# Squared lengths in column groups, an expert's weights held as the stationary operand, and norms of two chunks with a row moved ahead of the second attention

## The chip, the cores and the metric

The kernel runs on one core of one Trainium2 chip. The metric is the device time of one execution in microseconds, given as the median of its runs. PE is TensorE (PEld its weight loads), DVE is VectorE, ACT is ScalarE, POOL is GpSimd, SP is SyncE. A float32 matmul shows as two PE instructions ("passes") in the trace.

## What is computed

A decoder of two layers over x (2 x 512 tokens of 256 features, so 1,024 rows or 8 chunks of 128 rows) and a context of 2 x 1,024 rows of 128. Each step is added to x. Cut to its skeleton:

```
x += performer(ln(x))              # L0: 16 heads of 64, exp(dn*q@P.T - |q|^2*dn^2/2 - max)
x += causal_attn(ln(x)) + cross_attn(ln(x), ctx)
x += moe_top2_of_8(ln(x))
x += retention(ln(x))              # L1
x += double_attention(ln(x), ctx)  # a1 on itself, then a2 on the context, each with an MLP
x += moe_top1_of_4(ln(x))          # silu(x@w_v[gate]) * (x@w_v[value]) @ w_proj
```

In the performer each query and key needs its squared length per head. In the last step each row goes to the one expert whose router logit is highest. Between a1 and a2 stands `ln(x)` with a gain and a shift, and a2 begins with a layernorm of that result.

## The kernel before

Every stage is a class with one program for each engine. The order is written out by hand: a generator (`order`, `lead_in`) gives the steps, and each engine walks through the same steps and does its own part. Engines meet at semaphores; PSUM's eight banks are handed out in turn (`Banks.open`), and PE waits there until the earlier content of a bank has been read.

**Performer** (`Performer`, L503 to L925). Two heads make a pair; eight pairs for keys, eight for queries. `project` (L682) makes a pair's 128 features by 1,024 rows, ACT keeps them (L806) and their squares `sq` (L807). `tensor_features` multiplies by P (L695) and then makes the squared lengths (L701): eight matmuls whose stationary operand is a 128 x 128 chunk of `sq` and whose moving operand `half` has two columns, so that the result stands by rows, 16 columns in one bank. DVE copies it (L849), before the maxima of the same pair, and for queries forms maximum and exponent's argument (L894 to L899). ACT takes the exponential (L788), POOL adds a constant (L627), and PE turns the result (L361), multiplies by the contexts (L747). Between them stand `contexts` (L731) and `values` (L711).

**Lead-in of a2** (`Mha` with cross, L2283 ff.). a1 ends with an MLP: `tensor_up` (L2527) for the first and the second half of the rows, ACT's GELU (L2589), `tensor_row` (L2536), eight matmuls for a chunk of rows. Chunks 0 to 3 are made in a1's own program, chunks 4 to 7 in a2's lead-in, between a2's first maxima (L1282 on PE, L1402 on DVE: a matmul of 512 columns and the maximum over them, 37 of them and one set of turned maxima L1295 before the attention proper begins). Each row gets its add and its statistics on DVE (L425, L265), then, for four chunks at once, variance, root (L282 on ACT, which needs its table loaded between GELUs), gain and shift (L299, L301, one chunk of four on POOL), then the next layernorm (L265 to L297, L307). `xturn` (L361) turns four normed chunks, ACT copies them with gain and shift (L377), and the queries' projection (L1456) and its two copies (L1462, L1463) follow. How many maxima go behind each piece of the lead-in stands in `beside`.

**Last stage** (`Swiglu`, L3173 ff.). DVE ranks the rows by expert, POOL scatters them to DRAM (L3189, L3193, eight each), SP loads them back in 11 tiles of 128 rows, each tile owned by one expert. Per tile: two transposes (L3230), eight up matmuls of 512 columns with the tile's rows as the stationary operand and the owner's weights, found by a register, as the moving one (L3245); ACT silu (L3284), DVE product (L3310); eight transposes of the product (L3256), one half copied by DVE (L3324), the other by ACT (L3295); eight matmuls with `w_proj` (L3266) for the tile before.

## Time and profile before

| | us |
|---|---|
| median of 3 runs | 1690.67 |
| runs | 1687.85 to 1697.34 |
| the profiled execution | 1698.3 |
| its span, first to last instruction | 1696.5 |
| PE busy | 1558.7 (92%) |
| DVE busy | 855.4 (50%) |
| ACT busy | 694.0 (41%) |
| POOL busy | 565.0 (33%) |

The performer lies at 13 to 205 us of the span, the second attention's lead-in at 1147 to 1217 us, the last stage's tiles at 1558 to 1688 us. A PE that is busy is not yet at its full pace: the trace gives the granted clock beside the busy time, 1.00 for 2.4 GHz and 0.50 for 1.2 GHz, and at 0.50 every matmul takes twice as long.

### The profile page before, as it was taken

The page shows a single profiled execution, that of the slowest core. Times are in us where ns is not written, and L with a number is a line of the kernel's source. Part 1 is how long each engine was busy: PE and PEld are TensorE (multiplying, and loading weights), DVE is VectorE, ACT ScalarE, POOL GpSimd, SP SyncE. Part 2 cuts the span into 40 slices and gives each one's busy share as a digit, 9 for nine tenths or more (in the row PEclk, how much of TensorE's full clock was granted, in tenths as well). Part 3 has the DMA queues.
Part 4 walks back from the last instruction along what each step waited for, and adds up shares of the span by engine and source line. Part 5 has one row for each costly group of instructions (what it writes and reads, how often), then busy time and mean ns, then how long its engine had stood idle before and what let it go on. Part 6 is the DMA issues. An engine that isn't in the chain of part 4 may idle for free.

```text
span 1696.5 us, 24207 instructions
## 1 busy us (share of the span) xinstructions
PE 1558.7 (92%) x9698; PEld 821.3 (48%) x9711; DVE 855.4 (50%) x1797; ACT 694.0 (41%) x1015; POOL 565.0 (33%) x689
## 2 busy tenths in 40 slices
PE   7999989999999988798689999998799999994997
PEld 5788863333323363575363333564233333573565
DVE  2255547499947654101674567423677774212221
ACT  3443322567654534321315445541355556421111
POOL 3043233610105433000311346440367778603000
PEclk9999998999999988899789899997799999996999
DMA  6000010000000028542500000130300000373000
GB/s 198 1 1 1 1 47 7 1 1 1 1 1 1 1 80 290 169 163 68 78 2 19 0 1 2 51 112 0 118 1 1 1 1 25 107 285 120 7 11 8
DMA packets 70339, 84.24 MB, mean 50 GB/s; under 512 B 24945, under 2 KB 55889, under 8 KB 69202
## 3 DMA queue, kind: packets, MB, share of 16 engines
q1 hardware_dynamic: 67395, 75.31, 13.9%
q0 software_dynamic: 2832, 7.38, 1.4%
q8 instruction: 77, 1.26, 0.3%
q14 instruction: 35, 0.29, 0.1%
HBM read 63.56 MB, written 19.51 MB: 49 GB/s over the span
## 4 chain that ended last, share of the span: by engine, by line
PE 83%; DVE 6%; DMA 3%; ACT 3%; issue 2%; POOL 2%; SPq 0%; ACTq 0%; POOLq 0%; DVEq 0%
PE psum L1310 13%; PE psum L1329 9%; PE psum L1282 6%; PE psum L3245 5%; PE psum L2536 4%; PE psum L682 3%; PE psum L1306 3%; PE psum L1351 3%; PE psum L2527 3%; PE psum L2102 3%; PE psum L1456 3%; PE psum L3266 2%; DVE a_nm L1402 2%; PE psum L361 2%; PE psum L2094 2%
## 5 line engine op out<-in xcount | busy, mean ns | idle before, releaser
L1402 DVE TENSOR_REDUCE a_nm<-psum 128x1 f32<-128x512 f32 x384 | 251.2, 685 | 148.9 <-PE psum L1282 109.2
L1402 DVE TENSOR_REDUCE xa_nm<-psum 128x1 f32<-128x512 f32 x256 | 162.0, 683 | 31.2 <-PE psum L1282 25.4
L1364 ACT ACTIVATE xnT<-psum 128x1024 f32<-128x1024 f32 (+3 forms) x104 | 94.9, 952 | 64.7 <-PE psum L1310 55.1
L1364 ACT ACTIVATE a_w<-psum 128x1024 f32<-128x1024 f32 x86 | 83.8, 1021 | 66.5 <-PE psum L1310 56.4
L1310 PE MATMUL psum<-xa_cq,xa_ckT 32*128 32x512 f32 x512 | 104.1, 587 | 0.0
L1282 PE MATMUL psum<-a2kr,a2qr 32*128 32x512 bf16 x256 | 85.6, 402 | 16.5 <-DVE a_nm L1402 15.7
L1310 PE MATMUL psum<-a2qT,a2kT 32*128 32x512 f32 x512 | 97.9, 605 | 0.0
L1282 PEld LDWEIGHTS psum<-a2kr,a2qr 32*128 32x128 bf16 x256 | 21.0, 91 | 125.4 <-DVE a_nm L1402 111.0
L3245 PE MATMUL psum<-sw_wv,sw_xgT 128*128 x176 | 80.1, 609 | 0.5 <-ACT sw_xgT L3289 0.3
L1282 PE MATMUL psum<-xa_ckr,xa_cqr 32*128 32x512 bf16 x256 | 74.0, 390 | 2.9 <-POOL xa_ckr L1502 2.1
L1399 DVE TENSOR_REDUCE xa_parts<-psum 128x4 f32<-128x512 f32 x80 | 53.8, 690 | 43.0 <-PE psum L1277 23.2
L1364 ACT ACTIVATE xn<-psum 128x1024 f32<-128x1024 f32 (+3 forms) x64 | 56.5, 922 | 44.7 <-PE psum L1310 41.0
L1364 ACT ACTIVATE xa_w<-psum 128x1024 f32<-128x1024 f32 (+3 forms) x64 | 56.2, 915 | 37.4 <-PE psum L1310 33.6
L1306 PE MATMUL psum<-a_mrow,onesb 3*128 3x512 bf16 x384 | 69.9, 397 | 1.5 <-DVE a_mrow L1415 1.1
L1306 PE MATMUL psum<-xa_mrow,onesb 3*128 3x512 bf16 (+3 forms) x384 | 67.7, 357 | 3.3 <-ACT xa_w L1364 0.8
L3310 DVE TENSOR_TENSOR sw_h<-sw_gt,psum 128x512 f32<-128x512 f32 x22 | 15.1, 688 | 85.8 <-PE psum L3245 85.8
L2102 PE MATMUL psum<-mo_w,mo_hT 128*128 128x256 f32 (+1 forms) x256 | 58.0, 380 | 0.0
L1282 PEld LDWEIGHTS psum<-xa_ckr,xa_cqr 32*128 32x128 bf16 x256 | 19.1, 91 | 77.7 <-DVE xa_nm L1402 68.2
L1282 PE MATMUL psum<-a1kr,a1qr 32*128 32x512 bf16 x128 | 46.5, 408 | 8.1 <-DVE a_nm L1402 8.0
L2149 DVE COPY mo_o<-psum 128x256 f32<-128x256 f32 (+1 forms) x16 | 6.7, 418 | 93.0 <-PE psum L2103 93.0
L2037 POOL DMA_INDIRECT mo_xs<-scratch_yo,mo_fro x16 | 15.2, 950 | 115.2 <-issue 113.7
L622 POOL TENSOR_SCALAR pf_kdd<-pf_kdd 128x1024 f32<-128x1024 f32 x8 | 22.2, 2772 | 93.3 <-ACT pf_kdd L783 93.1
(528 smaller groups left out, 3356.6 us busy)
## 6 DMA issues: line engine op xcount, KB each, us to landing
mo_w<-in_L_ffn_W SPq DMA_DIRECT2D x16, 1024.0 KB, 7.4
sw_wv<-in_L_ffn_w_v SPq DMA_DIRECT2D x4, 2048.0 KB, 18.7
scratch_a2v<-co_v SPq DMA_DIRECT2D x16, 256.0 KB, 2.2
scratch_a2k<-co_k SPq DMA_DIRECT2D x16, 256.0 KB, 3.4
a2kT<-scratch_a2k SPq DMA_DIRECT2D x8, 512.0 KB, 8.3
a2v<-scratch_a2v SPq DMA_DIRECT2D x4, 1024.0 KB, 11.6
sw_wp<-in_L_ffn_w_proj SPq DMA_DIRECT2D x4, 1024.0 KB, 19.3
a1li<-in_L_xattn_a_li_w SPq DMA_DIRECT2D x2, 1024.0 KB, 6.4
```

What stands on the lines that cost most here:

```text
L682: t = e.matmul(k.ps[:, bank, :], wt[:, f, chunk(pair)], k.xnT[:, f, cols(n)], start=f == 0, stop=f == FC - 1)
L1282: t = e.matmul(out, query[:, chunk(i)], key[:, part * S:(part + 1) * S], start=True, stop=True)
L1306: e.matmul(ps[:, pr + h % 2, lo:S], self.k.const.onesb[rows, :], self.mrow[n % 3][rows, lo:S], start=True, stop=False)
L1310: t = e.matmul(ps[:, pr + h % 2, lo:S], job.key(h)[:, chunk(c)], job.query(h)[:, lo:S], start=False, stop=True)
L1329: t = e.matmul(ps[32 * h:32 * h + 32, 6, lo:hi], job.value(c, h), self.weights(n, c)[:, h, lo:hi], start=start, stop=last and not upper)
L1351: t = e.matmul(ps[32 * h:32 * h + 32, 7, :], self.k.const.ones[:, 0:32], self.weights(n, c)[:, h, :], start=(n, c) == self.dens(n)[0], sto ...
L1364: e.activation(self.weights(n, c)[:, 2 * jj:2 * jj + 2, lo:S], ps[:, pr:pr + 2, lo:S], ACT.Exp, scale=self.scale).then_inc(*self.weighed.m ...
L1399: e.tensor_reduce(self.parts[n % 3][:, q, part, :], view.rearrange("p (h n) -> p h n", n=P), AX.X, ALU.max, negate=True).then_inc(*self.ma ...
L1402: e.tensor_reduce(self.nm[n % 3][:, q, part, h:h + 1], view, AX.X, ALU.max, negate=True).then_inc(*self.max_taken.mark(*i))
L2102: e.matmul(ps[0:n, bank, 0:D], hT[:, m, lo:lo + n], w2[:, m, :], start=m == 0, stop=False)
L2536: t = e.matmul(self.k.ps[:, self.k.banks.of(self.rows.name, c), 0:D], self.hT[:, m, chunk(c)], self.li3[:, m, :], start=m == 0, stop=m == ...
L3245: t = e.matmul(k.ps[:, bank, :], self.xgT[:, i, chunk(f)], self.wv[:, bass.ds(owner, 1), f, off:off + BANK].rearrange("p o n -> p (o n)"), ...
```

## The change

Three edits.

**Squared lengths.** `half` gets 32 columns (two of them filled) and becomes the stationary operand; the squares are the moving one, 256 columns in each of four matmuls that write to four groups of 32 partitions. The result stands by heads, not by rows, so ACT copies it to SBUF (`scalar_diagonal`, in the steps `keys` and `queries`, ahead of what these did), PE turns it with two transposes (a new step, `turn_diagonal`, placed behind the next projection for keys and behind the contexts for queries), and DVE copies the turned form. For queries DVE does that between the first and the second instruction of the pair's chain.

```diff
-        for c in range(NC):
-            w.wait_ge(*self.squared.at(which, pair, c // 4))
-            t = e.matmul(k.ps[:, bank, 2 * c:2 * c + 2], self.sq[i][:, chunk(c)], self.half[:, :], start=True, stop=True)
+        for j in range(4):
+            w.wait_ge(*self.squared.at(which, pair, j // 2))
+            t = e.matmul(k.ps[32 * j:32 * j + 32, bank, 0:D], self.half[:, :], self.sq[i][:, j * D:(j + 1) * D], start=True, stop=True)
         t.then_inc(*self.diagonal.mark(which, pair))
+
+    def tensor_diagonal_turn(self, e, w, which, pair):
+        k, kept = self.k, self.diagT[self.turn_of(which, pair) % 2]
+        bank = k.banks.of("pf_diagonal", which, pair)
+        w.wait_ge(*self.diag_kept.at(which, pair))
+        for i in range(2):
+            t = e.transpose(k.ps[:, bank, D + i * P:D + (i + 1) * P], kept[:, chunk(i)], k.const.ident[:, :])
+        t.then_inc(*self.diag_turned.mark(which, pair))
...
             elif step == "queries":
                 q = self.qp[i % 3]
+                self.scalar_diagonal(e, w, "q", i)
                 for n in range(2):
                     w.wait_ge(*self.query_scaled.at(i, n))
...
@@ order
                 yield "queries", pair + 1
+                if pair == 0:
+                    yield "turn_diagonal", ("q", 0)
             yield "contexts", pair
+            if pair + 1 < PAIRS:
+                yield "turn_diagonal", ("q", pair + 1)
```

PE where the performer's queries begin (projection of pair 2, features and lengths of pair 1, contexts of pair 0, turn of its queries), before:

```order
L682 MATMUL psum<-xnT,pf_wq 128x512 x4
L695 MATMUL psum<-pf_pbd,pf_hT 128x128 x8
L701 MATMUL psum<-pf_half,pf_sq 128x2 x8
L731 MATMUL psum<-pf_v,pf_kdd 128x130 x8
L361 MATMUL psum<-ident,pf_qp 128x128 x8
```

and in the changed kernel:

```order
L695 MATMUL psum<-xnT,pf_wq 128x512 x4
L708 MATMUL psum<-pf_pbd,pf_hT 128x128 x8
L714 MATMUL psum<-pf_sq,pf_half 32x256 x4
L723 MATMUL psum<-ident,pf_diagT 128x128 x2
L753 MATMUL psum<-pf_v,pf_kdd 128x130 x8
L723 MATMUL psum<-ident,pf_diagT 128x128 x2
L361 MATMUL psum<-ident,pf_qp 128x128 x8
```

The turn of pair 0's lengths stands behind pair 1's features, that of pair 1's behind the contexts; PE did neither before.

ACT at the same place (exponentials of queries and keys, then the next pair's copies and squares), before:

```order
L788 ACTIVATE pf_qp<-pf_qp 128x1024
L783 ACTIVATE pf_kdd<-pf_kdd 128x1024
L806 ACTIVATE pf_hT<-psum 128x512
L807 ACTIVATE pf_sq<-psum 128x512
L806 ACTIVATE pf_hT<-psum 128x512
L807 ACTIVATE pf_sq<-psum 128x512
L788 ACTIVATE pf_qp<-pf_qp 128x1024
```

and in the changed kernel:

```order
L827 ACTIVATE pf_diagT<-psum 128x256
L812 ACTIVATE pf_qp<-pf_qp 128x1024
L806 ACTIVATE pf_kdd<-pf_kdd 128x1024
L838 ACTIVATE pf_hT<-psum 128x512
L839 ACTIVATE pf_sq<-psum 128x512
L838 ACTIVATE pf_hT<-psum 128x512
L839 ACTIVATE pf_sq<-psum 128x512
L827 ACTIVATE pf_diagT<-psum 128x256
```

The copy of pair 1's lengths stands behind the exponential of pair 0's queries, the keys' exponential and four copies.

**Last stage.** Before each tile ACT and DVE copy the owner's `w_v` (256 x 2,048, one half of the features each, 2,048 columns on 128 partitions) into one of two buffers (a new one and the space of `xnT` and `ctxT`). The up matmuls take chunks of it as the stationary operand and the tile's rows as the moving one, 32 matmuls of 128 columns. The result already stands by hidden features, so the eight transposes and their two copies go, and DVE's product is the projection's input.

```diff
-                for f in range(FC):
-                    t = e.matmul(k.ps[:, bank, :], self.xgT[:, i, chunk(f)],
-                                 self.wv[:, bass.ds(owner, 1), f, off:off + BANK].rearrange("p o n -> p (o n)"), start=f == 0, stop=f == FC - 1)
+                for j in range(4):
+                    features = slice(off + j * P, off + (j + 1) * P)
+                    for f in range(FC):
+                        t = e.matmul(k.ps[:, bank, chunk(j)], self.own[i % 2][f][:, features], self.xgT[i % 2][:, chunk(f)], start=f == 0, stop=f == FC - 1)
...
+    def copy_own(self, e, w, i, f, copy, done):
+        w.wait_ge(*self.owned.at())
+        owner = e.value_load(self.owner_i[0:1, i:i + 1], min_val=0, max_val=E1 - 1)
+        for x in range(E1):
+            w.wait_ge(*self.experts.loads[f"v{x}"].at())
+        if i > 1:
+            w.wait_ge(*self.up.at(i - 2, 1, "value"))
+        copy(self.own[i % 2][f], self.wv[:, bass.ds(owner, 1), f, :].rearrange("p o n -> p (o n)")).then_inc(*done.mark(i))
```

**Lead-in of a2.** The norms behind a1's MLP (`out_norm`) and ahead of a2 (`norm`) take two chunks at a time; all chunks of the first are applied by DVE and none by POOL. In ACT's program the root of chunks 0 and 1 stands ahead of the second half's first GELU, that of 2 and 3 behind it, and the next norm's roots and applications behind all eight GELUs (before, two were left). Chunk 4 of the rows is made ahead of the first turn, the last norm stands behind a query's projection, and `beside` deals out the maxima anew: 12 instead of 18 up to the last row, 14 instead of 8 behind the last query.

```diff
-        pieces[4:4] = [("turn", 1)]
-        pieces[1:2] = [("row", (c, m)) for c in range(SC, NC) for m in range(HC)] + [pieces[1], ("norm", 4)]
-        return [("turn", 0)] + list(self.attention.lead_in(pieces, 0, 0, self.beside))
+        rows = lambda c: [("row", (c, m)) for m in range(HC)]
+        pieces[1:4] = rows(5) + rows(6) + [("norm", 4)] + rows(7) + [pieces[1], ("norm", 6), *pieces[2:4], ("turn", 1)]
+        return rows(4) + [("turn", 0)] + list(self.attention.lead_in(pieces, 0, 0, self.beside))
...
+        if step[0] == "row":
+            return step[1][1] % 2 if step[1] < (NC - 1, 4) else 0
+        if step[0] == "query":
+            return 2 if step[1] == (0, 0) else 3 * step[1][1]
+        return 2 if step[0] == "turn" else 0
```

PE in the second part of the lead-in (last rows, queries, second turn, up to the turned maxima), before:

```order
L2536 MATMUL psum<-a1li,a1hT 128x256
L1456 MATMUL psum<-xnT,a2wq 128x512 x4
L1282 MATMUL psum<-a2kr,a2qr 128x512 x2
L1456 MATMUL psum<-xnT,a2wq 128x512 x2
L1282 MATMUL psum<-a2kr,a2qr 128x512 x2
L361 MATMUL psum<-ident,ctxT 128x128 x8
L1282 MATMUL psum<-a2kr,a2qr 128x512
L1456 MATMUL psum<-xnT,a2wq 128x512 x2
```

and in the changed kernel:

```order
L2585 MATMUL psum<-a1li,a1hT 128x256 x4
L1491 MATMUL psum<-xnT,a2wq 128x512 x6
L361 MATMUL psum<-ident,ctxT 128x128 x8
L1317 MATMUL psum<-a2kr,a2qr 128x512 x2
L1491 MATMUL psum<-xnT,a2wq 128x512 x2
L1317 MATMUL psum<-a2kr,a2qr 128x512 x3
L1491 MATMUL psum<-xnT,a2wq 128x512 x2
L1317 MATMUL psum<-a2kr,a2qr 128x512 x3
```

The four maxima between the first half's queries are gone, and the second half's queries have three behind each instead of two.

ACT between the second half's first GELU and the first turn's copies, before:

```order
L2589 ACTIVATE a1hT<-psum,cols 128x512 x2
L282 ACT_TABLE_LOAD
L282 ACTIVATE a_norm_std<-a_norm_std 128x4
L2589 ACT_TABLE_LOAD
L2589 ACTIVATE a1hT<-psum,cols 128x512 x4
L282 ACT_TABLE_LOAD
L282 ACTIVATE a_norm_std<-a_norm_std 128x4
L307 ACTIVATE ctxT<-xn,a_norm_std 128x256 x2
L2589 ACT_TABLE_LOAD
L2589 ACTIVATE a1hT<-psum,cols 128x512 x2
```

and in the changed kernel:

```order
L2638 ACTIVATE a1hT<-psum,cols 128x512
L282 ACT_TABLE_LOAD
L282 ACTIVATE a_norm_std<-a_norm_std 128x2
L2638 ACT_TABLE_LOAD
L2638 ACTIVATE a1hT<-psum,cols 128x512 x7
L282 ACT_TABLE_LOAD
L282 ACTIVATE a_norm_std<-a_norm_std 128x2 x2
L307 ACTIVATE ctxT<-xn,a_norm_std 128x256 x2
```

No table load stands ahead of the last two GELUs any more.

## Rows read from the trace of the kernel before

**Rows 1.** Busy time of the engines in one stretch, with TensorE's granted clock.

```profile
89.00:200.00 111.00, 110.73 (x857) 99.01 (x856) 65.91 (x173) 42.84 (x68) 41.56 (x15) 1.00 0.00 1
```

**Rows 2.** PE timeline, one pair of the first attention's queries (start, us, engine, line).

```profile
123.37 1.95 PE L695 MATMUL psum<-pf_pbd,pf_hT 128*128 128x128 f32 x16
125.15 1.84 PE L701 MATMUL psum<-pf_half,pf_sq 128*128 128x2 f32 x16
126.86 2.04 PE L731 MATMUL psum<-pf_v,pf_kdd 128*128 128x130 f32 x16
128.73 1.91 PE L361 MATMUL psum<-ident,pf_qp 128*128 128x128 f32 x16
130.48 3.74 PE L711 MATMUL psum<-pf_wv,xnT 128*128 128x128 f32 x32
134.05 1.95 PE L747 MATMUL psum<-pf_bd,pf_qpT 128*128 128x130 f32 x16
```

**Rows 3.** PE timeline of the third attention: four column groups, and what follows.

```profile
983.59 0.64 PE L1329 MATMUL psum<-xnT,a1v 128*32 128x256 f32 x8
984.17 0.39 PE L1282 MATMUL psum<-a1kr,a1qr 32*128 32x512 bf16 x1
```

**Rows 4.** DVE timeline in the same pair as rows 2.

```profile
127.04 0.17 DVE L849 COPY pf_diag<-psum 128x16 f32<-128x16 f32 x1 [4.48 <-PE psum L701]
...
131.80 0.68 DVE L384 COPY pf_qpT<-psum 128x512 f32<-128x512 f32 x1
```

**Rows 5.** Timeline of DVE, POOL and ACT where the queries begin.

```profile
92.49 1.23 DVE L879 SCALAR_TENSOR_TENSOR pf_kdd<-pf_kdd,pf_diag 128x1024 f32<-128x1024 f32 x1
93.55 2.80 POOL L627 TENSOR_SCALAR pf_qp<-pf_qp 128x1024 f32<-128x1024 f32 x1 [5.79 <-ACT pf_qp L788]
93.75 1.06 ACT L783 ACTIVATE pf_kdd<-pf_kdd 128x1024 f32<-128x1024 f32 x1 [0.28 <-DVE pf_kdd L879]
...
95.19 0.59 ACT L807 ACTIVATE pf_sq<-psum 128x512 f32<-128x512 f32 x1
```

**Rows 6.** PE timeline of the second attention's lead-in.

```profile
1150.10 1.53 PE L361 MATMUL psum<-ident,ctxT 128*128 128x128 f32 x8 [2.98 <-ACT a1hT L2589]
1152.59 3.75 PE L1456 MATMUL psum<-xnT,a2wq 128*128 128x512 f32 x4 [0.96 <-ACT xnT L377]
...
1159.26 2.07 PE L2536 MATMUL psum<-a1li,a1hT 128*128 128x256 f32 x4
...
1171.60 1.13 PE L2536 MATMUL psum<-a1li,a1hT 128*128 128x256 f32 x4
...
1197.74 1.20 PE L1282 MATMUL psum<-a2kr,a2qr 32*128 32x512 bf16 x2 [6.00 <-DVE a_nm L1402]
...
1217.25 0.61 PE L1295 MATMUL psum<-identb,a_np 128*128 128x128 bf16 x4
```

**Rows 7.** ACT timeline in that lead-in.

```profile
1150.82 1.63 ACT L377 ACTIVATE xnT<-psum,cols 128x512 f32<-128x512 f32 x2 [0.77 <-PE psum L361]
```

**Rows 8.** Busy time and clock in three stretches, columns as in rows 1.

```profile
1156.00:1171.00 15.00, 14.31 (x30) 6.96 (x29) 5.60 (x9) 2.37 (x3) 0.00 (x0) 0.50 0.00 0
...
200.00:206.00 6.00, 4.53 (x30) 3.71 (x31) 3.08 (x10) 2.24 (x3) 0.00 (x0) 1.00 0.00 0
619.00:623.00 4.00, 2.55 (x14) 1.57 (x13) 2.35 (x7) 1.16 (x3) 0.22 (x1) 0.82 0.00 0
```

**Rows 9.** Chain that ended last, in order of time: a tile of the last stage.

```profile
1649.83 6.87 PE psum L3245 x16
1656.70 3.45 PE psum L3266 x16
1661.24 6.87 PE psum L3245 x16
```

**Rows 10.** PE timeline, the last tile's projection.

```profile
1684.07 3.72 PE L3266 MATMUL psum<-sw_wp,sw_hT 128*128 x16 [0.43 <-DVE sw_hT L3324]
```

**Rows 11.** POOL timeline, the first of eight row scatters ahead of the last stage.

```profile
1541.43 1.12 POOL L3189 DMA_INDIRECT scratch_swx<-xn,sw_to  x1 [7.26 <-DVE sw_owner L3380]
```

More of the change, by code:

```diff
@@ L303, in scalar_apply @@
     def scalar_apply(self, e, w, g):
-        for c in range(g, g + 4):
+        for c in range(g, g + self.size):
             if self.of(c) in "ab":
@@ L311, in pool_apply @@
         step = self.k.pool
-        for c in range(g, g + 4):
+        for c in range(g, g + self.size):
             dst = self.dst[:, c, :]
```

152 lines of the change are left out of this document (81 added, 71 removed).

## The prediction, on record before the changed kernel ran

> **What bounds the kernel now.** I read the page first: PE is busy for 92% of the span, so a microsecond counts where PE works or waits. Then busy time and clock by stretch, since a busy PE at 0.50 does half the work: in the performer's queries PE is busy 110.73 of 111.00 us at 1.00 [rows 1], so there every pass that goes is won and every new wait is lost. In the second attention's lead-in it is waits and the clock: PE waits 2.98 us for a GELU and 0.96 us for the turned chunks [rows 6], then does 15 us at 0.50 [rows 8], and later waits 6.00 us for DVE, which has all four chunks' norms ahead of the maxima [rows 6]. In the last stage the chain runs on PE alone, a tile every 1661.24 - 1649.83 = 11.41 us [rows 9].
>
> **Squared lengths, the pass itself.** Now 126.86 - 125.15 = 1.71 us a pair [rows 2]. The nearest row to the new form is a value product of four column groups with 256 columns: eight passes, and the next instruction starts 0.58 us later [rows 3]; so the groups run beside each other. A transpose costs (130.48 - 128.73) / 16 = 0.11 us [rows 2], two 0.22. New 0.80, saved 0.91, over 16 pairs **14.6 us**. If the groups ran one after another, eight passes of 256 columns at 3.72 / 16 = 0.23 us [rows 10] make 1.86, with the turn 2.08, and 16 pairs would lose 5.9 us; that end of the bounds is far from rows 3.
>
> **Its new waits.** PE's turn waits for ACT's copy, and DVE's chain for the turn. For keys the turn is a projection (3.5 us) behind, and ACT's copy, shorter than the 0.59 of 512 columns [rows 5], is done: no wait. For a query pair in the steady state, counted from the start of its features [rows 2]: features to 1.78, lengths to 2.36, contexts to 4.1, turn to 4.36, sixteen transposes to 6.1, values to 9.7; there `output` needs DVE's copy of the turned queries. Before, DVE's chain began at 127.04 - 123.37 = 3.67 and that copy ended at 132.48, 9.1 [rows 4]. Now the chain begins at about 4.55, its first maximum (0.6) done already, so the copy ends at 3.67 to 4.55 later less 0.6, about 9.4, and PE wants it at 9.7 instead of 134.05 - 123.37 = 10.7. It fits, with 0.3 us left.
>
> The **first query pair** doesn't fit. Its turn stands behind pair 1's features, and DVE's chain, ACT's exponential and everything that ACT has behind it hang on it. From that turn's end: DVE's chain for both halves 2.8 us; ACT's exponential 1.06 beside DVE's scaling of the next keys (0.23 + 1.23, done at 4.3); ACT's keys' exponential 1.06 to 5.4; four copies and squares at some 0.5 to 7.4; the copy of pair 1's lengths 0.4 to 7.8 [rows 5]. PE has only the contexts, 1.8 us, until it needs that copy. So PE stands for about **6.0 us**, once. POOL's 2.80 [rows 5] ends inside it. After a stand of that length the clock is likely to be at 0.50: after the 6.00 us wait it was at 0.50, and in the lead-in it took work of several us to come back [rows 6, 8]. Passes of some 5 us at 0.50 cost **2.7 us** more (bounds 0 and 7, half the 15 us of rows 8). The performer: 14.6 - 6.0 - 2.7 = **5.9 us** saved.
>
> **Last stage.** The eight transposes of a tile go: 8 x 0.11 = 0.88 us, 11 tiles, 9.7 us, and at the end the 0.43 us in which PE waits for a copy of the last [rows 10]. The up matmuls stream the same columns in 64 passes of 128 instead of 16 of 512. The same alternation of a new 128 x 128 stationary chunk and 128 moving columns is in `values`: (134.05 - 130.48) / 32 = 0.112 us a pass [rows 2], 64 make 7.14 against 6.87 [rows 9], 0.27 a tile, 3.0 us in all. Left: 9.7 + 0.4 - 3.0 = 7.1. No row shows a copy of 2,048 columns: ACT's 1,024 take 1.06 [rows 5], so some 2.0, DVE's 1,024 with two operands 1.23, so at most 2.4. A tile lasts 10.8 us, and each buffer is free for one whole tile ahead: hidden. The first two copies of DVE fall where POOL issues the eight scatters that PE waits for, and the first of those, beside small DVE work, took 1.12 us [rows 11]. Bounds 0 and 2 x 2.4 = 4.8 us; I take 1.5, since the copies are two and not all of each hits a scatter. Last stage **5.6 us** saved.
>
> The Trainium skill, SBUF — State Buffer, "SBUF: two separate sides", says more sharply that a float32 `tensor_copy` of VectorE from SBUF to SBUF keeps GpSimd from writing its DMA descriptors until it ends. By that rule both copies would be paid whole and, by their length at one column a cycle, the scatters come up to 4.8 us late; I keep it as a rival.
>
> **Lead-in.** From PE's end of the second up projection (1150.10 - 2.98 = 1147.12) to the turned maxima (1217.25) it now takes 70.1 us [rows 6]. The new course at clock 1.00: ACT has no table load ahead of its last GELUs any more, so the last follows PE's end by its own length and a hop, about 0.9 us (512 columns take 0.59 without a function's extra [rows 5]); row 3.5; the first norm, from DVE and ACT, is ready as the row ends; turn 0.9; ACT's two copies (1.63, the first beside the turn [rows 7]) leave a wait of 1.35; query 1.8; its copy 0.75: 9.2 us. Then two maxima, ten groups of two row matmuls and a maximum at 1.38 (1.13 and what follows [rows 6]) and four row matmuls, 16.1; DVE's gain and shift for two chunks hold up its maxima by 1.9 once. Three queries 5.4, a wait of 1.2 for the last norm, turn and two maxima 1.5, a wait of 0.8. Four queries with three maxima each: the third waits for a bank, 3.3 us each, 13; then 14 maxima at DVE's pace of 0.6 (0.68 for 512 columns [rows 4], a little overlapped), 8.4. Sum 57 us, 13 saved. The clock takes some back. At the second turn PE waits, turns and waits again as before, and will do some 7 us at 0.50, 3.5 us. At the first turn it is open: waits of 0.9, 1.35 and 0.75 with eight transposes between. Of two stretches with transposes between short waits, one fell (619 to 623, mean 0.82) and one held (200 to 206, 1.00) [rows 8]. If it falls there, rows and maxima run at 2.5 us a group (2.07 and its maximum [rows 6]) instead of 1.38, five or six groups long, 6 us. So 10 us saved if it holds, **4 us** if it falls. I take the fall, since three waits follow each other here.
>
> **Sum.** 5.9 + 5.6 + 4 = 15.5 us: 1682.8 against the profiled execution's 1698.3, and **1675.2** against the median of 1690.67, since the profiled run lay 7.6 above it and nothing in the sum is a share of the time.
>
> **Rivals.** (a) The clock holds at the first turn: 10 instead of 4, **1669**. For it: no wait is over 1.4 us, against 2.98 now. (b) DVE's later chain is seen in every query pair, not in one alone: only 0.3 us is left, and with 0.9 us more in the strided copy or in semaphores PE waits in 7 pairs, 6 us, **1681**. Against it: hops in rows 2 and 4 are about 0.2. (c) DVE's copies hold POOL whole (4.8 instead of 1.5) and the lead-in gives nothing, since its 14 last maxima are DVE's and the clock is low: 5.9 + 2.3 + 0, **1682.5**. (d) On the other side: the column groups don't run beside each other. Its place is L714, its price 16 x (2.08 - 0.80) = 20.5 us, **1696**; it decides from about 1.7 us a pair for lengths and turn, where the performer's gain is gone and the 8.7 of the first pair stay. Against it stand rows 3. (e) The change does less than it says: the first query pair costs more than is won in all, say 15 us of stand and low clock: 1681.5.
>
> **How the numbers follow.** Forecast (the fall at the first turn) 0.42, 1670 to 1680; (a) 0.27; (b) 0.10; (c) 0.10; (d) 0.05; (e) 0.06. Within 0.5% (8.5 us, about what a measurement of this kernel can tell from no change) are 1682.2 to 1699.1: half of (c), part of (b) and (e) and of (d), with some spread of the median; over that a part of (d). Faster 0.81, same 0.15, slower 0.04. The range takes in (a) with POOL unhindered below and (c) with a worse clock above: 1663 to 1687.
>
> **What would show it.** In the changed kernel's trace: lengths start 0.58 us ahead of the next PE instruction; one PE wait of about 6 us (on ACT) behind the contexts of pair 0 and no others in the performer; key pairs at 6.1 us instead of 7.0, query pairs at 15.0 instead of 15.9; tiles at 10.8 us; scatters longer than now only under DVE's copies; the wait of 2.98 gone to below 1 us, that of 6.00 to about 1.2; the clock in the first rows at 0.50 (forecast) or 1.00 (a). Wrong would be: waits in each query pair, tiles above 11.4, or a lead-in of 70 us.

## The result, and the profile after

The changed kernel's median is **1674.95 us** (1663.90 to 1689.80, 20 runs) against 1689.26 us of the kernel before beside it (1683.65 to 1699.57, 20 runs). The ratio of the two is 0.9909, with a 95% interval of 0.9886 to 0.9933: 15.4 us less, and 1675.2 was predicted. The profiled execution took 1671.95 us with a span of 1670.2 us, 26.3 us less than the span before. Runs at a low clock that lie over 1.5% above the fastest of their kernel (one here, three of the joined kernel's twelve in experiment 1, one of ten in experiment 4) are kept in the medians and means below; without its one the median here is 1674.69 us.

So the two traces show 26 us and the medians 14 to 15. That gap is the first thing to explain, for a sum that comes out right may hold terms that don't. I cut both traces at the same landmarks and read length and granted clock of every stage. Four stages are touched:

| stage | before, us | after, us | saved | forecast |
|---|---|---|---|---|
| performer, 0 to the projection behind it | 239.0 | 233.2 | 5.8 | 5.9 |
| lead-in, from the MLP's start to a2's attention | 114.2 | 104.6 | 9.6 | 4 |
| last stage, from the first up projection to the end | 138.1 | 128.6 | 9.5 | 5.6 |
| all others | 1205.2 | 1203.8 | 1.4 | 0 |

(The 5.6 holds 1.5 us for POOL's scatters, which lie ahead of that stretch; for the stretch itself the sum had 7.1.)

**Performer.** First the PE timeline of the changed kernel where the queries begin and in a later pair (start, us, engine, line, output and inputs, count; in brackets idle time before it and what ended it).

```profile
87.63 0.44 PE L723 MATMUL psum<-ident,pf_diagT 128*128 128x128 f32 x2
89.26 2.06 PE L753 MATMUL psum<-pf_v,pf_kdd 128*128 128x130 f32 x16 [1.19 <-DVE pf_qp L934]
...
95.49 0.44 PE L723 MATMUL psum<-ident,pf_diagT 128*128 128x128 f32 x2 [4.17 <-ACT pf_diagT L827]
...
96.82 5.19 PE L733 MATMUL psum<-pf_wv,xnT 128*128 128x128 f32 x32
101.85 1.95 PE L769 MATMUL psum<-pf_bd,pf_qpT 128*128 128x130 f32 x16
...
107.07 1.95 PE L708 MATMUL psum<-pf_pbd,pf_hT 128*128 128x128 f32 x16
108.95 0.64 PE L714 MATMUL psum<-pf_sq,pf_half 128*32 128x256 f32 x8
109.52 2.06 PE L753 MATMUL psum<-pf_v,pf_kdd 128*128 128x130 f32 x16
...
122.17 1.95 PE L708 MATMUL psum<-pf_pbd,pf_hT 128*128 128x128 f32 x16
```

The lengths are followed 0.57 us later by the next instruction (108.95 to 109.52), as [rows 3] had it, where [rows 2] show 1.71; the turn behind the contexts takes 0.22. A pair lasts 122.17 - 107.07 = 15.10 us. Against that stand one wait of 4.17 us on ACT's copy of the lengths and one of 1.19 us on DVE, 5.4 in all. Behind them the turn of eight chunks takes 0.18 us longer, and the values 101.85 - 96.82 = 5.03 instead of 3.57: the clock fell to half there and cost 1.6 us. No other full pair waits. One price is hidden in these rows: the features ahead of the lengths now take 108.95 - 107.07 = 1.88 us, where [rows 2] have 125.15 - 123.37 = 1.78. So a pair is 0.81 us shorter and not 0.91, 13.0 us in all instead of 14.6, and 13.0 - 5.4 - 1.6 = 6.0 us is what the stage shows (5.8). This is ACT's timeline at that place, with the first and the last of what stands in front of the copy, the keys' exponential and four copies and squares:

```profile
90.82 1.06 ACT L812 ACTIVATE pf_qp<-pf_qp 128x1024 f32<-128x1024 f32 x1 [8.66 <-DVE pf_qp L934]
...
93.12 0.58 ACT L838 ACTIVATE pf_hT<-psum 128x512 f32<-128x512 f32 x1
...
95.03 0.41 ACT L827 ACTIVATE pf_diagT<-psum 128x256 f32<-128x256 f32 x1
```

**Lead-in.** PE's timeline of the changed kernel, which answers [rows 6]:

```profile
1140.52 3.72 PE L2585 MATMUL psum<-a1li,a1hT 128*128 128x256 f32 x16 [0.78 <-ACT a1hT L2638]
...
1149.27 1.13 PE L2585 MATMUL psum<-a1li,a1hT 128*128 128x256 f32 x4
...
1150.65 1.13 PE L2585 MATMUL psum<-a1li,a1hT 128*128 128x256 f32 x4
...
1159.00 0.38 PE L1317 MATMUL psum<-a2kr,a2qr 32*128 32x512 bf16 x1 [1.71 <-DVE a_nm L1437]
...
1173.53 1.07 PE L361 MATMUL psum<-ident,ctxT 128*128 128x128 f32 x6 [1.34 <-DVE ctxT L297]
...
1177.21 3.75 PE L1491 MATMUL psum<-xnT,a2wq 128*128 128x512 f32 x4 [2.29 <-ACT xnT L377]
...
1200.26 0.61 PE L1330 MATMUL psum<-identb,a_np 128*128 128x128 bf16 x4
```

The wait of 2.98 us is 0.78, that of 6.00 has become two, of 1.71 and 1.34, and a group of two row matmuls and a maximum takes 1150.65 - 1149.27 = 1.38 us from the first one on: the clock did not fall at the first turn. From the second up projection's end to the turned maxima it is 1200.26 - 1139.74 = 60.5 us instead of 70.1. One wait is larger than planned: 2.29 us on the second turn's copies. ACT's timeline shows why:

```profile
1173.18 0.60 ACT L307 ACTIVATE ctxT<-xn,a_norm_std 128x256 f32<-128x256 f32 x1 [0.96 <-DVE a_norm_std L290]
1173.69 0.58 ACT L1497 ACTIVATE a2qr<-psum 128x512 bf16<-128x512 f32 x1
...
1175.60 1.47 ACT L377 ACTIVATE xnT<-psum,cols 128x512 f32<-128x512 f32 x2
```

The copies of two finished queries (L1497, L1498) stood in ACT's queue behind the application of the last norm (L307), which itself waited for DVE, and the turn's copies (L377) behind them.

**Last stage.** The chain of work that ended last in the changed kernel, in order of time (start, us, engine, what, line, count), which answers [rows 9]:

```profile
1561.05 7.15 PE psum L3295 x64
1571.87 7.15 PE psum L3295 x64
...
1654.54 6.92 PE psum L3306 x32
```

The timeline of the changed kernel with the first of DVE's two copies and POOL's scatters beside it, which answers [rows 11]:

```profile
1525.83 1.40 POOL L3240 DMA_INDIRECT scratch_swx<-xn,sw_to  x1 [0.31 <-issue]
1525.89 1.23 DVE L3334 COPY sw_own<-sw_wv 128x2048 f32 x1 [1.24 <-issue]
...
1527.54 1.55 POOL L3240 DMA_INDIRECT scratch_swx<-xn,sw_to  x1 [0.30 <-issue]
1529.39 0.96 POOL L3240 DMA_INDIRECT scratch_swx<-xn,sw_to  x1 [0.30 <-issue]
```

A tile takes 1571.87 - 1561.05 = 10.82 us against 11.41 in [rows 9], and the last two projections follow each other without a wait. The two scatters under DVE's copies took 1.40 and 1.55 us, one beside nothing 0.96. ACT's own copy of 2,048 columns took 1.91 us and DVE's 1.23, which was at most 2.4 in my bounds. The scatter of 1.40 us ends at 1527.23, 0.11 us after DVE's copy beside it (1525.89 + 1.23 = 1527.12).

### The profile page after: what moved, and what is told of

Same layout as the page of the kernel before. It is cut to its first block, busy times and chain, and to the rows that moved or that the text cites. A ratio compares the mean times of both kernels' runs of the same rounds, so it can differ in the third digit from the quotient of the medians.

```text
span 1670.2 us, 24916 instructions
## 1 busy us (share of the span) xinstructions
PE 1529.4 (92%) x10055; PEld 831.6 (50%) x10055; DVE 861.7 (52%) x1811; ACT 713.0 (43%) x1035; POOL 564.7 (34%) x683
## 4 chain that ended last, share of the span: by engine, by line
PE 84%; DVE 7%; ACT 3%; issue 2%; DMA 2%; POOL 1%; DVEq 0%; POOLq 0%; ACTq 0%; SPq 0%
PE psum L1345 13%; PE psum L1364 9%; PE psum L1317 6%; PE psum L3295 5%; PE psum L695 4%; PE psum L2585 3%; PE psum L1341 3%; PE psum L2576 3%; PE psum L1386 3%; PE psum L2137 3%; PE psum L1491 3%; DVE a_nm L1437 2%; PE psum L3306 2%; PE psum L2129 2%; PE psum L733 2%
## 5 line engine op out<-in xcount | busy, mean ns | idle before, releaser
L1345 PEld LDWEIGHTS psum<-xa_cq,xa_ckT 32*128 32x128 f32 x512 | 50.1, 193 | 3.2
L2159 ACT ACTIVATE mo_hT<-psum,cols 128x154 f32<-128x154 f32 x64 | 21.4, 386 | 70.6 <-PE psum L2129 70.6
L1399 ACT ACTIVATE ctxT<-psum 128x1024 f32<-128x1024 f32 x40 | 38.9, 1021 | 29.1 <-PE psum L1345 24.1
```

The costliest lines, as they stand in the source:

```text
L1345: t = e.matmul(ps[:, pr + h % 2, lo:S], job.key(h)[:, chunk(c)], job.query(h)[:, lo:S], start=False, stop=True)
L1399: e.activation(self.weights(n, c)[:, 2 * jj:2 * jj + 2, lo:S], ps[:, pr:pr + 2, lo:S], ACT.Exp, scale=self.scale).then_inc(*self.weighed.m ...
```

## Experiment 1: each edit alone

Three kernels, each the kernel before with one of the three edits as shown in the section on the change, and the changed kernel beside them on the same chip, so that all share the 35 runs of the kernel before (median 1691.77 us).

> The squared lengths' edit alone, on the kernel before. My sum has 5.9 us saved: 14.6 for 16 pairs, less one stand of some 6 us at the first query pair and 2.7 us of work at half clock behind it; the changed kernel's own trace shows 5.4 us of waits and some 1.7 us of half clock there, so 7.5 us by those rows. If instead each pair's passes save less than they seem, because DVE's and ACT's work is the limit, the whole gain is under 3 us and waits stand in the query pairs.

> The last stage's edit alone. My sum has 5.6 us saved. The two profiled executions put the stretch from 0.1 us ahead of the first up projection to the end at 9.5 us less, so the rival theory is that the gain is some 9 us: 11 tiles at 0.6, the last hidden turn's 0.9 and 0.4, 1.3 at the first tile and 1.5 between the first two. By the first theory POOL's two held scatters take 1.0 to 1.5 us of it back, by the second they only take 0.5.

> The lead-in's edit alone. My forecast had 4 us saved with the clock at half after the first turn, the rival 10 us with the clock held. The changed kernel's trace shows the clock held and 9.6 us. If the held clock belongs to this edit, the rows of chunks 5 to 7 run at 1.00 here too and 9 to 10 us are saved; if it was luck of that one execution (a clock that holds in some and falls in others), they run at 0.50 and about 4 us are saved.

> The changed kernel with all three edits, on the same chip as the three alone. If the edits don't meet, its saving is the sum of the three alone; by my sum 15.5 us, by the traces of stretches 7.5 + 9.5 + 9.6 = 26.6 us, by the medians of 20 runs 14.3 us. A sum of the three alone well over the joined one would show that one edit's gain is given back where another is made.

| kernel | median, us | ratio to before | 95% interval |
|---|---|---|---|
| lengths alone | 1690.95 | 0.9993 | 0.9972 to 1.0015 |
| last stage alone | 1681.79 | 0.9934 | 0.9913 to 0.9956 |
| lead-in alone | 1691.85 | 1.0000 | 0.9972 to 1.0028 |
| joined | 1677.38 | 0.9917 | 0.9883 to 0.9952 |

Only the last stage gives about what its stretch shows (8 to 11 us; the expectation of 9 holds against my 5.6, which lies outside the interval of 7.4 to 14.7). The lengths give 1 us where the stretch in their own trace is 5 us shorter, and the lead-in none, though its trace has the same 104.6 us as the changed kernel. Something outside the edited code takes the gain back. By the ratios the three alone add up to 12.3 us and the joined kernel saves 14.0 (8.1 to 19.8), so no gain is lost where the edits meet, and the 26.6 us of the stretches are not there.

## What takes the gains back: the clock in stages that nobody touched

Each run comes with the mean granted clock of its span, and within one kernel the times follow it closely: through all kernels that were timed, 0.01 of clock goes with 14.2 us (a line with one slope for all; 13.2 in the kernel before alone). So I compare the kernels once as they are and once at the same clock, 0.948, by that slope:

| kernel | mean, us | mean clock | at 0.948, us | difference at 0.948 |
|---|---|---|---|---|
| before (three sets, 80 runs) | 1689.7 to 1691.3 | 0.9485 to 0.9493 | 1691.6 to 1692.0 | 0 |
| lengths alone | 1690.8 | 0.9441 | 1685.3 | -6.6 |
| last stage alone | 1681.4 | 0.9497 | 1683.9 | -8.0 |
| lead-in alone | 1690.0 | 0.9495 | 1692.1 | +0.2 |
| changed kernel (20 and 12 runs) | 1675.6, 1680.4 | 0.9485, 0.9450 | 1676.3, 1676.1 | -15.7 |

The 95% intervals of the fourth column are 0.5 to 1.1 us wide on either side. At equal clock the lengths save 6.6 us, close to the 5.9 of the sum; the clock then takes most of it back. The lead-in is the opposite: its stretch has the clock at 0.85 before and at 0.94 after, so what it saves there is largely clock itself, and nothing is left at equal clock. (The comparison has a bias: idle time at half clock lowers the mean too, so a kernel with more of it looks a little better in the last column than it is. Experiment 4 has the size: 5.4 us more of waiting show as 2.3 at equal clock. The new lead-in has less waiting, so its +0.2 is likely too high.)

Where the clock differs, the traces show stage by stage. To see which stages move without any edit, I profiled the kernel before a second time.

> The kernel before once more, for a second trace of the same code. Its first trace lay 7.6 us above its median. If that is the clock in stages that the change doesn't touch, this trace differs from the first by whole steps in some of them (the attention's entry 75.0 or 68.8 us, the expert tiles 125.2 or 127.7, retention 73.4 or 75.5), each with its clock, and not in the others; if it is a drift of everything, all stages differ by the same share.

Busy time by stretch (from : to, us, then busy us of PE, PEld, DVE, ACT, POOL with instructions, clock, DMA). The kernel before, first trace: entry of the third step, expert tiles, last stage.

```profile
238.98:313.96 74.98, 72.08 (x201) 27.99 (x201) 56.48 (x129) 21.32 (x33) 32.91 (x51) 0.88 0.12 30
692.89:818.38 125.49, 106.80 (x573) 78.42 (x573) 22.72 (x51) 27.92 (x74) 13.26 (x14) 0.92 0.34 111
1558.43:1696.50 138.07, 128.68 (x458) 78.83 (x458) 27.43 (x45) 24.55 (x44) 13.33 (x14) 0.96 0.08 27
```

The same three stretches in the second trace of that kernel:

```profile
239.58:308.40 68.82, 66.19 (x199) 26.52 (x200) 55.80 (x129) 21.24 (x33) 32.90 (x51) 0.97 0.14 33
688.56:816.29 127.73, 109.08 (x572) 80.82 (x573) 22.73 (x51) 27.98 (x74) 13.28 (x14) 0.90 0.34 108
1555.74:1692.30 136.56, 127.18 (x458) 78.39 (x458) 27.42 (x45) 24.55 (x44) 13.71 (x14) 0.97 0.09 29
```

The same code took 74.98 us at 0.88 or 68.82 us at 0.97; 125.49 at 0.92 or 127.73 at 0.90; 138.07 at 0.96 or 136.56 at 0.97; and all 288.8 us of the attention between them are equal to 0.1 us. So these are whole steps in single stages, as the first theory had it, and no drift. The other traces take the same steps: retention 73.4 (0.92) or 75.4 (0.88), a1's attention 136.5, 138.0 or 140.0. Retention and the first attention (288.8 to 291.8) take their steps with and without the edits alike. Two steps go mostly with the lengths' edit, though it touches no line there. The expert tiles are at 127.5 us or more in nine of ten traces that have it, and at 125.1 to 125.5 in three of four without it: some 2 us given back for the 5.8 won. And the old lead-in takes 111.6 us in both traces with it, 114.2 or 114.3 in the three without: as much won again. The largest step of all, the entry's 6.1 us, is at its high level in two of four traces without the lengths' edit, in five of seven with it, and in none of the three with the earlier turn of experiment 2. That may be a part of it, but with so few traces it is a suspicion; what takes the lengths' gain back stays open.

**The lead-in's courses.** With the new lead-in the clock held through the rows in three traces (104.6 us each). In two (106.2 us each) it fell behind DVE's wait of 1.71 us for some 4 us, so that the next two groups of row matmuls took 1.87 and 1.76 us instead of 1.13. In two others with the same lead-in code (111.3 and 111.4) it fell there and stayed at half to the last row. The old one took 114.2, 114.2, 114.3, 111.6 and 111.6. Here is one that fell, PE's timeline of the first kernel of experiment 4:

```profile
1162.86 0.39 PE L1317 MATMUL psum<-a2kr,a2qr 32*128 32x512 bf16 x1 [1.71 <-DVE a_nm L1437]
...
1164.88 2.08 PE L2585 MATMUL psum<-a1li,a1hT 128*128 128x256 f32 x4
...
1167.41 2.08 PE L2585 MATMUL psum<-a1li,a1hT 128*128 128x256 f32 x4
```

The code up to here is that of the changed kernel and so is every wait before it (0.78, 1.19, 0.69, 1.71), yet from 1163 on two row matmuls and a maximum take 1167.41 - 1164.88 = 2.53 us instead of 1.38. And the attention behind it suffers too. In the changed kernel's trace and then in this one, 16 and 36 us at the place where the lead-in ends and the attention begins, and the whole attention (columns as above):

```profile
1196.00:1212.00 16.00, 14.50 (x62) 5.33 (x63) 10.25 (x18) 3.98 (x4) 7.87 (x13) 0.50 0.00 1
1201.78:1437.96 236.18, 227.29 (x1792) 74.77 (x1785) 157.18 (x254) 132.50 (x143) 176.92 (x164) 0.98 0.02 6
```

```profile
1206.00:1242.00 36.00, 33.54 (x143) 10.83 (x147) 20.65 (x33) 9.91 (x10) 16.90 (x20) 0.50 0.00 1
1212.44:1456.25 243.81, 234.55 (x1792) 75.91 (x1785) 157.51 (x254) 132.49 (x143) 176.94 (x164) 0.94 0.02 5
```

The first stretch of each is at 0.50. The changed kernel leaves half clock some 11 us into the attention and needs 236.2 us for it, as the kernel before does; this one stays there until 1242 and needs 243.8. So the best course saves 9.6 us, and the worst saves 2.8 and loses 7.6: 5 us slower than the kernel before. (The two losses need not come together: in experiment 6 the clock fell in the rows to their end, and the attention took 236.3 us.) From 1691.3 the best and the worst course make 1681.7 and 1696.1, and the twelve runs of the lead-in alone split in just that way, six from 1676.8 to 1689 (mean 1684) and six from 1694 to 1700.5 (mean 1696). I have a trace of the first kind of this kernel and of the second kind only of kernels with the other edits beside it, so that the split has this cause is likely and not shown. What decides which course an execution takes stays open.

**From 26 to 15.** The two profiled executions differ by 26.3 us. Of that, 1.5 is the last stage's step and 4.8 are those of retention and what follows it, both high in the first trace of the kernel before; 3.1 went the other way, the first attention's 291.8 in the changed kernel. The expert tiles were at 125.2 in the changed kernel's trace, where nine of ten have 127.5 or more: 2.5. The lead-in is at 104.6 and keeps its pace behind, where the mean over seven traces is 107.0 and (243.8 + 240.8 - 2 x 236.2) / 7 = 1.7 in the attention, against 113.2 with the old lead-in instead of 114.2: a saving of 4.5 instead of 9.6, 5.1 less. 26.3 - 1.5 - 4.8 + 3.1 - 2.5 - 5.1 = 15.5, where the ratio gives 15.4. I chose these steps knowing what had to come out, and retention's is as high in the second trace of the kernel before, so this is a plausible account and no proof.

## Experiment 2: an earlier turn for the first query pair

```diff
                 if pair + 2 < PAIRS:
                     yield "project", ("q", pair + 2)
-                yield "queries", pair + 1
                 if pair == 0:
                     yield "turn_diagonal", ("q", 0)
+                yield "queries", pair + 1
```

> The changed kernel with the first query pair's turn of lengths ahead of pair 1's features instead of behind them. My theory of the stand: DVE's chain and all that ACT has behind it hang on that turn, so with the turn 2.4 us (features and lengths) earlier and those 2.4 us of work to lie beside the chain, the stand of 5.4 us shrinks by 2.4 + 0.2 to some 3 us, and with it the half clock behind it: 3 to 4 us faster than the changed kernel. The rival: the stand belongs to ACT's queue itself (copies and squares of pair 2 ahead of the copy of pair 1's lengths), and stays at 5 us wherever the turn is.

> The squared lengths' edit alone, with the first query pair's turn earlier. The edit alone gave 0.8 us where I had 5.9. Theory one: the performer's stage gives what its trace shows (6.0 us at the start, 1.8 given back at the queries), and the rest is lost to lower clocks in later stages whose code is the same (2.3 us in the expert tiles); with the stand 2.7 us shorter this one gains 2.7 to 3.5 us more, 1687. Theory two: the stand itself is nothing that the time sees, because something later absorbs it; then it stays at 1691.

Once in the changed kernel: median **1668.04 us**, ratio to before 0.9896 (0.9874 to 0.9918), and at equal clock 3.1 us below the changed kernel. Once with the lengths alone: 1685.98 us, ratio 0.9974 (0.9948 to 0.9999) instead of 0.9993 (3.2 us), at equal clock 2.9 us less, so theory two (nothing moves) is unlikely. PE's timeline of the first of the two:

```profile
93.08 0.69 PE L723 MATMUL psum<-ident,pf_diagT 128*128 128x128 f32 x2 [3.08 <-ACT pf_diagT L827]
...
95.26 4.10 PE L733 MATMUL psum<-pf_wv,xnT 128*128 128x128 f32 x32
99.20 1.95 PE L769 MATMUL psum<-pf_bd,pf_qpT 128*128 128x130 f32 x16
```

One wait of 3.08 us in place of 4.17 + 1.19, and values in 3.94 us instead of 5.03, with 128.5 us for the queries instead of 131.2. The stand is real, it hangs on the turn's place as the sum had it, and the rival (it stays wherever the turn is) has fallen. What is left of it is ACT's queue: exponential, exponential, four copies and squares, then the copy of pair 1's lengths.

## Experiment 3: the column groups

```diff
-            t = e.matmul(k.ps[32 * j:32 * j + 32, bank, 0:D], self.half[:, :], self.sq[i][:, j * D:(j + 1) * D], start=True, stop=True)
+            t = e.matmul(k.ps[0:32, bank, 0:D], self.half[:, :], self.sq[i][:, j * D:(j + 1) * D], start=True, stop=True)
```

> The changed kernel with all four matmuls of the squared lengths written to the same 32 partitions instead of to four groups, so that they can't run beside each other; three quarters of the lengths are then lost and the output is wrong in that part. By my bounds the eight passes last 1.86 us one after another instead of 0.57: 1.3 us more a pair, 16 pairs, 20 us slower, and the key pairs last 7.4 instead of 6.2. If the 0.57 came from something else than the groups (32 columns of stationary operand that load quickly), the passes stay near 0.6.

PE's timeline of this kernel, the lengths of a query pair and what follows:

```profile
98.74 1.91 PE L714 MATMUL psum<-pf_sq,pf_half 128*32 128x256 f32 x8
100.58 0.44 PE L723 MATMUL psum<-ident,pf_diagT 128*128 128x128 f32 x2
```

The same eight passes last 1.84 us (98.74 to 100.58) when they write to one group and 0.57 when they write to four, and nothing else differs. The bound for the rival of serial groups was 1.86. The key pairs together took 78.8 us instead of 68.4 and the queries 141.4 instead of 131.2, 20.6 us in all where 20.5 was its price. The one run took 1708.94 us, 34 us above the changed kernel's median; the rest of that lies in the clock's steps of other stages, the attention's 240.8 us among them.

## Experiment 4: DVE's copies and POOL's scatters

```diff
         self.vector_places(e, w)
+        w.wait_ge(*self.loads["scatter"].at(NC - 1))
         self.vector_own(e, w, 0)
```

The second kernel puts eight more copies of the same size ahead of DVE's own, back to back:

```diff
     def vector_own(self, e, w, i):
+        if i == 0:
+            ...
+            for n in range(8):
+                w.wait_ge(*self.k.vec.now())
+                e.tensor_copy(self.own[1][1], self.wv[:, 0, 1, :]).then_inc(*self.k.vec.mark())
```

> The changed kernel with DVE's first two copies of weights held until the eight scatters have landed. If the copies cost the scatters 0.44 + 0.59 us, these take 0.96 to 1.1 each again, the first tile's turn comes 1.0 us earlier against POOL's first scatter (15.5 us as in the kernel before, not 16.0 to 16.5), and the kernel is 1 us faster or the same within the measurement. If it was something else that made two scatters long, they stay long and nothing moves. The copies then end some 1 us ahead of the first turn, so no wait is added.

> The changed kernel with eight more copies of 2,048 columns on DVE ahead of its first two, back to back: extra work that leaves the result alone. DVE then copies for about 12 us beside POOL's eight scatters. If a copy holds POOL until it ends, as my rival (c) and the Trainium skill's page SBUF — State Buffer have it, no scatter ends while copies follow each other (or one slips in between two copies, 1.2 us each at least), and the first tile's turn comes some 8 to 11 us later. If a scatter under a copy takes 0.44 to 0.59 us longer, as two did in the changed kernel's trace, eight or so are 0.5 longer: 3 to 4 us later. Each us of that is a us of the time.

POOL's and DVE's timeline in the first kernel, a scatter ahead of the copies and one beside them:

```profile
1546.37 0.96 POOL L3240 DMA_INDIRECT scratch_swx<-xn,sw_to  x1 [0.30 <-issue]
...
1556.48 1.45 POOL L3244 DMA_INDIRECT scratch_swr<-x,sw_to  x1 [0.30 <-issue]
1556.59 1.23 DVE L3334 COPY sw_own<-sw_wv 128x2048 f32 x1 [12.67 <-issue]
```

DVE's and POOL's timeline in the second kernel, where ten copies lie beside the scatters:

```profile
1516.64 10.06 DVE L3346 COPY ctxT<-sw_wv 128x2048 f32<-128x2048 f32 x8
1518.29 2.22 POOL L3240 DMA_INDIRECT scratch_swx<-xn,sw_to  x1 [0.31 <-issue]
...
1530.53 0.96 POOL L3240 DMA_INDIRECT scratch_swx<-xn,sw_to  x1 [0.30 <-issue]
```

With the copies behind, the scatters take 0.96, and those two of the next eight that now lie beside the copies take 1.45 and 1.69. From POOL's first scatter to PE's turn it is 15.10 us instead of 16.02: the two copies cost 0.9 us. The other traces agree: 15.99 to 16.08 in six with the copies beside the scatters, 14.90 to 15.10 in six without, and only the first trace of the kernel before stands apart with 15.54. The medians (1675.39 us, ratio 0.9924, 0.9901 to 0.9947; at equal clock 0.9 us less) agree and can't prove it. With ten copies the same stretch is 21.39 us: 6.3 for ten copies of 1.26, half of each. The three scatters that lie wholly under the eight added copies (one row is shown; the group of copies is one row of 10.06 us) take 2.22 us each instead of 0.96, one copy more. So a scatter is held while a copy runs and gets on where two copies meet. Where scatters end says the same: 1556.48 + 1.45 is 0.11 us after the end of the copy at 1556.59, and in the changed kernel it was 0.11 too. The median of that kernel is 1682.20 us, ratio 0.9972 (0.9943 to 1.0002), at equal clock 2.3 us above the changed kernel: less than the stretch's 5.4, by the bias named above. Neither number of the expectation fits: 5.4 us later lies between 3 to 4 and 8 to 11.

The Trainium skill, SBUF — State Buffer, "SBUF: two separate sides", says that GpSimd can't write its DMA descriptors during such a copy of VectorE. The mechanism fits these rows; its price is not the copies' whole length but 0.9 of 2.5 us in the changed kernel. The prediction had doubled the copies' length (4.8 us for both). That a scatter writes only in a part of its time would explain the rest; no run here shows that.

## Experiment 5: the wait ahead of row 4

```diff
-        self.scalar_hidden(e, w, 1, range(1, HC))
+        self.scalar_hidden(e, w, 1, range(1, HC - 2))
         if self.next:
             self.next.scalar_ahead(e, w)
+        self.scalar_hidden(e, w, 1, range(HC - 2, HC))
```

> The changed kernel with ACT's last two GELUs of the second half behind the next norms' roots and applications again, as in the kernel before: a table load and its return ahead of them. PE then waits for the last GELU some 3 us instead of 0.8 ahead of row 4. My theory of the clock: it held in the changed kernel because no wait there is longer than 1.2 us, so with a 3 us wait it falls and the rows and maxima up to the queries run at 2.5 us a group instead of 1.38: 2.2 us of wait and about 6 us of clock, 8 us slower. The rival: the clock held for another reason (row 4 ahead of the turn is work that keeps it), then only 2.2 us.

The median is 1689.38 us (1687.52 to 1696.26, 11 runs), ratio to before 0.9998 (0.9980 to 1.0016): 14.4 us above the changed kernel, and the whole gain is gone with two GELUs. PE's timeline of this kernel, row 4 and two of the rows' groups:

```profile
1148.09 5.41 PE L2585 MATMUL psum<-a1li,a1hT 128*128 128x256 f32 x16 [3.06 <-ACT a1hT L2639]
...
1158.52 1.13 PE L2585 MATMUL psum<-a1li,a1hT 128*128 128x256 f32 x4
...
1159.90 1.13 PE L2585 MATMUL psum<-a1li,a1hT 128*128 128x256 f32 x4
```

Its busy time and clock, first the lead-in, then the attention behind it:

```profile
1102.47:1217.10 114.63, 99.07 (x294) 50.76 (x296) 50.22 (x130) 39.88 (x62) 20.80 (x29) 0.86 0.26 85
1217.10:1461.04 243.94, 234.67 (x1791) 75.93 (x1785) 157.54 (x254) 132.50 (x143) 176.88 (x164) 0.94 0.02 5
```

The wait is back (3.06 us), and the clock fell at once, in row 4 (5.41 us instead of 3.72), but it was back at 1.00 with the first turn, and the rows' groups took 1159.90 - 1158.52 = 1.38 us. So my expectation of slow rows was wrong. The clock fell again behind the 1.71 us wait, for 4 us, and at the second turn; there it stayed at half until 1203 and not for 7 us as in the changed kernel. It was at 1.00 from 1203 to 1210, and at half once more until 1248, 31 us into the attention: 114.6 us instead of 104.6 and 243.9 instead of 236.2, 17.8 us in this trace. (The profiled execution was the slowest of the eleven.) At equal clock this kernel lies 2.0 us above the changed one, its wait of 2.28 us and nothing more; its mean clock is 0.9396 against 0.9485 and 0.9450, in all eleven runs 0.935 to 0.943. A wait of 2.3 us thus costs 14: in the changed kernel 8 of 32 lay above 1684 us, here all do. That those 8 took the bad course is likely; none of them has a trace. Both theories fall in part: the long wait does cost clock, but not where I said.

## Experiment 6: four small edits together

The early turn, the copies behind the scatters, and in the lead-in the last norm's step one query later and four maxima behind the second turn instead of two:

```diff
-        pieces[1:4] = rows(5) + rows(6) + [("norm", 4)] + rows(7) + [pieces[1], ("norm", 6), *pieces[2:4], ("turn", 1)]
+        pieces[1:4] = rows(5) + rows(6) + [("norm", 4)] + rows(7) + [*pieces[1:3], ("norm", 6), pieces[3], ("turn", 1)]
...
-        return 2 if step[0] == "turn" else 0
+        return 4 if step[0] == "turn" else 0
```

> The changed kernel with four small edits: the first query pair's turn of lengths earlier (2.7 us less of a stand, measured in a trace), DVE's first two copies of weights behind the scatters (0.9 us), in the lead-in the last norm's step behind the third query instead of the second (ACT then copies a query ahead of that norm and the second turn's copies start earlier: PE's wait of 2.29 us there falls to some 1.3), and four maxima instead of two behind the second turn, so 12 instead of 14 at the end at DVE's 0.6 (about 1 us). Sum 5.5 us below the changed kernel, 1670. The rival theory is the clock's: what matters is whether the clock is held in the lead-in and comes back early in the attention behind it, worth 7 and 8 us; then the median lies at 1665 where most executions have the good course and at 1680 or more where few have.

Median **1670.29 us** (1664.19 to 1677.22), ratio to before 0.9880 (0.9849 to 0.9912), at equal clock 4.1 us below the changed kernel. PE's timeline of this kernel behind the second turn, a maximum and the next query:

```profile
1178.22 0.38 PE L1317 MATMUL psum<-a2kr,a2qr 32*128 32x512 bf16 x1 [0.78 <-DVE a_nm L1437]
...
1179.35 3.78 PE L1491 MATMUL psum<-xnT,a2wq 128*128 128x512 f32 x4
```

The wait of 2.29 us for ACT is gone: between turn and query lie the maxima, with 0.78 and 0.21 us of waiting for DVE. In this trace the clock fell in the rows (109.8 us for the lead-in instead of 104.6, at 0.88), so the lead-in's part of the edit can't be read from the time, and that the expectation of 1670 was met says little of its terms. The early turn alone (1668.04) and the four together (1670.29) can't be told apart by their six runs each; both beat the changed kernel's 1674.95, and at equal clock the four are 1 us ahead, within the intervals.

## Why the prediction was right, and where it wasn't

- **Total.** 15.5 us forecast, 15.4 by the ratio. The sum was made as fixed terms, and the transfer to the median (7.6 us off the profiled run) was right: the second trace of the kernel before has the differences in stages with unchanged code.
- **Squared lengths, the pass itself.** 0.57 + 0.22 us instead of 0.58 + 0.22, and experiment 3 shows the reason, with 1.84 us for the other end of the bounds: (d) has fallen. But the term of 14.6 was 13.0. It left out that the features ahead of the lengths take 1.88 us instead of 1.78; key pairs are at 6.2 us and query pairs at 15.10, both 0.1 above what was forecast.
- **First query pair.** 6.0 us of stand were 5.4, in two waits and not one, since the contexts also wait, by the profile, for DVE's first read of the query features (`pf_qp`, L934); 2.7 us of half clock were 1.6. The performer's 5.9 is 5.8, by three errors that cancel (1.6 too much won, 0.6 and 1.1 too much lost). (e) has fallen. Not foreseen: what the clock takes back outside the stage, so that the lengths alone give 0.8 us in the median (5.9 lies outside their interval of -4.7 to +2.5).
- **Steady query pairs.** "It fits, with 0.3 us left": no pair waits. (b) has fallen.
- **Last stage.** The tile's 10.8 was right (10.82). The term of 5.6 was too small: the edit alone gave 10 in the median and 8.0 at equal clock. From the first up projection to the end five traces with the old form have 136.6 to 138.1 us, nine with the new one 128.5 to 130.1, on average 8.0 less, where the sum had 7.1 without the copies. Of the 8.0, 6.9 lie behind the first projection, the same in every trace; the first two tiles give 1.1 on average and move with the clock. (The two profiled runs alone have 9.5, since the kernel before had its slowest start there.) And POOL's 1.5 was 0.9. (c) has fallen in size, while its mechanism is there.
- **Lead-in.** The step that failed is "I take the fall, since three waits follow each other here". At the first turn the clock fell in none of the traces. It held through the rows in three of seven, where 9.6 us were saved and rival (a) had said 10; it fell for a moment behind DVE's wait of 1.71 us in two (8.0 saved), and to the end of the rows in two (2.8 saved). The average over the seven is 6.2, and 1.7 of it is given back in the attention, which no rival named: 4.5. So the 4 is near that average for a wrong reason, by luck; the lead-in alone gave 0 in the median, with an interval of 4.7 to either side, so its runs don't settle it. The sum itself was 0.9 too high in any case: its terms add up to 57.5 and 3.5 us, 9.1 saved and not 10, and 3.1 with the fall. The second turn's wait was 2.29 us instead of 0.8: I had not counted ACT's four query copies behind the norm's application.
- **Errors that met.** The last stage gave 2 to 4 us more than its term, and the clock elsewhere took back as much from the lengths. The total is better than its parts, and that it came within 0.1 us is luck.

## What to carry to other kernels

Cut two traces of the same kernel at the same landmarks before you trust one of them: whole stages step by 2 to 8 us with the clock, and an edit may move such a step in a stage that it doesn't touch (likely here, not shown). Report an edit's gain as the mean of many runs, with the mean clock beside it, and compare at equal clock too, as a hint at what the edited code itself gives; waits can show too small there. Where short waits lie ahead of a long dense stage, as here, test a wait of 2 or 3 us for the clock behind it and don't price it by its length (here 2.3 us were 14). And a step that is moved joins a queue: look at every engine's order for what then stands behind it.

## What the runs showed that I had not expected

- Two executions of the same lead-in code with the same waits had the clock at 1.00 and at 0.50 in the same rows, and left half clock 11 or 30 us into the attention.
- After a 3.06 us wait the clock was back at 1.00 after 5.4 us of row matmuls; in the changed kernel waits of 1.34 and 2.29 us on either side of the second turn had it at 0.50 for 7 us.
- The lead-in's mean clock rose from 0.85 to 0.94 in the traces, yet the mean clock of that kernel's runs did not rise (0.9485 both).
- Eight passes of 256 columns cost 0.57 us in four column groups and 1.84 in one.
- A row scatter takes 0.96 us by itself, 1.40 to 1.69 beside one copy of 1.23 us and 2.22 under an unbroken row of them; one that a copy holds can end 0.11 us behind that copy.
- The features' 16 passes take 1.88 us ahead of the four column groups and 1.78 ahead of the old lengths.
